# Two causal self-attentions: unread TensorE products ahead of the first transposes and ahead of the first softmax's transposes

## The reference, cut to what matters

```python
def _L0_attn_ref(x, qkv_w, qkv_b, out_w, out_b):
    qkv = (x @ qkv_w + qkv_b).reshape(b, s, 3, h, hd)          # h = 16, hd = 32, s = 64
    q, k, v = (qkv[:, :, 0], qkv[:, :, 1], qkv[:, :, 2])
    logits = jnp.einsum('bqhd,bkhd->bhqk', q, k)
    logits = jnp.where(causal_mask, -jnp.inf, logits) * scale
    att = jax.nn.softmax(logits, axis=-1)
    out = jnp.einsum('bhqk,bkhd->bqhd', att, v).reshape(b, s, d)
    return out @ out_w + out_b

x = x + _L0_xattn_ref(ctx_768, _layernorm(x, axis=-1), ...)    # stage a
x = x + _L0_attn_ref(_layernorm(x, axis=-1), ...)              # stage b
x = x + _L0_ffn_ref(_layernorm(x, axis=-1), ...)               # stage c
x = x + _L1_xattn_ref(_layernorm(x, axis=-1), ctx_768, ...)    # stage d
x = x + _L1_attn_ref(_layernorm(x, axis=-1), ...)              # stage e
x = x + _L1_ffn_ref(_layernorm(x, axis=-1), ...)               # stage f
```

## Time and profile before

| what | us |
|---|---|
| median of 3 runs | 2872.34 |
| these runs | 2870.62 to 2891.36 |
| the profiled execution, its time | 2867.43 |
| the profiled execution, its span | 2865.7 |
| stage b, first statistics to the barrier after it | 1096.6 to 1204.1 |
| stage e, the same | 2290.3 to 2392.8 |

### The profile page before, as it was taken

The page is one execution under the profiler, slowest core; times in us unless marked ns, Lnnn a source line. Parts: engine busy times, 40 slices in busy tenths (PEclk is TensorE's granted clock), DMA queues, the critical chain, the costliest instruction groups (busy, mean ns, idle before and its releaser), DMA issues. The chain is left out here.

```text
span 2865.7 us, 29255 instructions
## 1 busy us (share of the span) xinstructions
PE 2401.2 (84%) x10384; PEld 1468.5 (51%) x10384; DVE 1206.3 (42%) x2242; ACT 738.2 (26%) x1476; POOL 588.5 (21%) x530
## 2 busy tenths in 40 slices
PE   5588988879879778589999977775998776999998
PEld 2435545546456324444444434454464344887886
DVE  4865665665566202410000158775571243311312
ACT  1335334343253200211111134333261012000000
POOL 0330321312303000069997112121000000000000
PEclk9799999999999989689999988776999986998999
DMA  2101101101000031267888463321400012244241
GB/s 79 58 1 49 49 0 48 49 0 48 15 35 11 0 143 66 72 261 303 310 311 318 167 213 111 103 97 36 184 15 0 5 57 120 118 179 172 117 176 73
DMA packets 100219, 298.75 MB, mean 104 GB/s; under 512 B 35824, under 2 KB 63889, under 8 KB 82449
## 3 DMA queue, kind: packets, MB, share of 16 engines
q1 hardware_dynamic: 96096, 285.88, 27.1%
q10 hardware_dynamic: 2736, 7.41, 0.7%
q0 software_dynamic: 1280, 4.20, 0.4%
HBM read 279.05 MB, written 17.30 MB: 103 GB/s over the span
## 5 line engine op out<-in xcount | busy, mean ns | idle before, releaser
L728 PE MATMUL a_mix<-a_probs_T,a_xn 128*128 128x512 f32 (+1 forms) x624 | 271.8, 596 | 5.3 <-ACT a_latent_probs L612 5.3
L425 POOL TENSOR_TENSOR a_xn<-a_xn,a_gain 128x1536 f32<-128x1536 f32 (+1 forms) x32 | 90.4, 2825 | 617.3 <-DVE a_xn L479 616.7
L1514 PE MATMUL c_gate_up<-c_w_wide,c_h_rows 128*128 128x512 f32 x480 | 210.9, 592 | 0.0
L728 PEld LDWEIGHTS a_mix<-a_probs_T,a_xn 128*128 128x128 f32 (+1 forms) x624 | 118.6, 191 | 155.5 <-issue 155.5
L1419 DVE TENSOR_TENSOR c_hidden<-c_silu,c_gate_up 128x512 f32<-128x512 f32 x38 | 26.1, 688 | 353.8 <-PE c_gate_up L1514 343.5
L111 PE MATMUL a_ks<-a_wk_high,a_xn_high 128*128 128x512 f32 x312 | 134.3, 431 | 23.3 <-DVE a_xn_low L459 23.3
L479 DVE TENSOR_SCALAR a_xn<-a_xn,a_mv,a_rstd 128x384 f32<-128x384 f32 (+1 forms) x104 | 146.6, 1465 | 1.2
L1514 PEld LDWEIGHTS c_gate_up<-c_w_wide,c_h_rows 128*128 128x128 f32 x480 | 90.1, 190 | 108.1 <-issue 108.1
L1830 PE MATMUL f_ring<-f_hidden,f_w 128*128 128x160 f32 x1024 | 141.2, 300 | 3.1 <-ACT f_hidden L1758 3.1
L1830 PEld LDWEIGHTS f_ring<-f_hidden,f_w 128*128 128x128 f32 x1024 | 139.3, 190 | 5.1 <-ACT f_hidden L1758 5.1
L1819 PE MATMUL f_ring<-f_picked_T,f_w 128*128 128x160 f32 x1024 | 140.4, 299 | 0.0
(11 more groups left out here) (451 smaller groups left out, 4275.6 us busy)
## 6 DMA issues: line engine op xcount, KB each, us to landing
c_w_wide<-in_L_ffn_W SPq DMA_DIRECT2D x68, 1024.0 KB, 6.9
f_w<-in_L_ffn_W SPq DMA_DIRECT2D x16, 4096.0 KB, 12.0
c_w_down<-in_L_ffn_W SPq DMA_DIRECT2D x34, 1024.0 KB, 7.5
a_xn<-in_ctx SPq DMA_DIRECT2D x24, 768.0 KB
d_context_T<-in_ctx_T SPq DMA_DIRECT2D x24, 768.0 KB, 10.7
d_context<-in_ctx SPq DMA_DIRECT2D x8, 2304.0 KB
mixed_context<-a_mixed SPq DMA_DIRECT2D x24, 256.0 KB, 3.3
a_mixed<-mixed_context SPq DMA_DIRECT2D x1, 6144.0 KB
```

The costliest lines, as they stand in the source:

```text
L425: pool.tensor_tensor(part, part, gain[0:m].unsqueeze(1).to_broadcast([m, hi - lo, DC]), ALU.mult).then_inc(pool_own, 1)
L728: last = pe.matmul(mix[f][:], xn[0:m, par, t, f * P:(f + 1) * P], probs_T[0:m, t, :], start=(t == 0), stop=(t == CT - 1))
L1514: last = pe.matmul(gate_up[2 * (u % 2) + part][:], h[:, k, :], w_wide[:, i % WIDE_RING, k, :], start=(k == 0), stop=(k == KD - 1))
```

## The change

A helper on TensorE issues n products of the identity (stationary, 128 x 128) with `g.hT[:, 0, :]` (moving, 512 columns, float32) into one PSUM bank, each with start and stop set, with no semaphore wait and no signal. Seven stand ahead of the wait for the norm, into `ring[3]`; six stand behind both `pair_scores` calls and ahead of the wait for tile 0's probabilities, into the bank that tile 0's value products write later. Nothing reads either result. Both attentions get them.

```diff
         @block.tensor
         def _(pe):
+            def keep_running(n, out):
+
+                for _ in range(n):
+                    pe.matmul(out, g.ident[:], g.hT[:, 0, :], start=True, stop=True)
+
+            keep_running(7, flat(ring[3]))
             pe.wait_ge(norm.normed, NT)
...
             pair_scores(0)
             pair_scores(1)
             for t in range(NT):
+                if t == 0:
+                    keep_running(6, flat(ring[(R_TILE + 3) % 4]))
                 pe.wait_ge(probs_ready, t + 1)
```

## The result

The changed kernel takes 2885.02 us (median of 20 runs, 2873.45 to 2901.53), the kernel before 2871.5 (20 runs, 2860.99 to 2891.36): ratio 1.0046, 95% interval 1.0028 to 1.0063, that is +13 us with +8 to +18 in the interval. The profiled execution has a span of 2880.5 us. The forecast was 2879.0, +6.7 us: the direction is right, and the size lies just under the interval.

A forecast was written before the change was run, and what follows sets the result against it. TensorE, busy for 84% of the span, was taken to set the time; norms -0.6 (b) and +1.5 (e) and softmaxes +2.9 and +2.9 sum to +6.7 us, from median 2872.34 to 2879.0, range 2870 to 2889.

The forecast's parts named there:

- What one call costs: An added float32 matmul call on TensorE is two instructions: 0.86 us at full clock, 1.71 at half.
- When the clock rises: TensorE's clock reaches full after 2.8 to 5.9 us of work at half clock, middle 4.3.
- Part 1: Stage b's norm: seven calls start at full clock, end 0.6 us late, faster transposes give 1.2 back: -0.6 us.
- Part 2: Stage e's norm: seven calls start at half clock and overrun the gap: +0.8 to +2.35 us, taken as +1.5.
- Parts 3 and 4: Softmaxes of stages b and e: six calls overrun a 2.94 us gap before tile 0's transposes: +2.9 us each.
- I give nothing for tile 1: Softmax, tile 1's transposes: clock falls in some 4.5 us of idle, so no gain; bound -0.9 us each stage.
- A: Rival: the full clock, once reached, holds through the softmax; not slower, -3.3 us, 2869.0; chance 0.12.
- B: Rival: added products do not raise the clock and run at half level throughout; +20.6 us, 2892.9; chance 0.04.
- C: Rival: each added call is one instruction, so the change costs half; -0.85 us, 2871.5; chance 0.04.
- A rule weighed: Norm's transposes: a skill text says transposes don't engage the full clock; the forecast rejected it on the trace; no size.
- nothing for the start of the output projection: Output projection's start, 3.3 us at half clock in stage b: no change counted, may shift either way by 1.6 us.

The follow-up runs named there:

- x2: The changed kernel with the seven norm products taken out, so only the six softmax products stay; ratio 1.0034 against the kernel before.
- x1: The changed kernel with the six softmax products taken out, so only the seven norm products stay; ratio 1.0037 against the kernel before.

## Why the prediction was right, and where it was too low

- What one call costs (two instructions, 0.86 us at full clock, 1.71 at half): right. 52 records more, 6.25 us for fourteen instructions at full clock, 8.61 from half clock, 4.9 and 5.1 us for six more calls.
- When the clock rises, 2.8 to 5.9 us of work with 4.3 as the middle: 4.7 us in e's norm (the level is 0.50 from 2299.0 to 2303.7), and in b's softmax 3.8 us after the calls start (1156.49 to 1160.3), 3.2 forecast. Right.
- Part 1, b's norm, -0.6: -0.6 and, over two profiles each, -0.8. Right for the norm; alone it gives ratio 1.0001, and the stage as a whole is no shorter.
- Part 2, e's norm, +1.5: +1.4. The products ended 8.45 us after the statistics, 8.15 forecast. That the weights' landing would have taken any gain is shown by the run with three calls.
- Parts 3 and 4, +2.9 in each softmax: by VectorE's wait +3.2 and +2.9 in the profile, +2.5 and +2.9 in the second. To the output projection it is +3.05 in b and +2.05 in e, where the level rose ahead of the last tile's transposes (1.09 us, 1.97 before) and gave 0.9 back. Right.
- "I give nothing for tile 1": right, its wait is 2.06 in every execution with the change or with twelve calls.
- The rivals. A fell: the level dropped in the idle behind tile 0, even after twelve calls. What A described is real when the gaps are filled too, and worth 7 us. B fell, as tile 0's transposes ran at full clock; its ground, that 512-column products raise the level "everywhere", was drawn from one place, the output projection of b. C fell by the count.
- "A rule weighed": the window behind the earlier trace rows, in which the last transposes end and no other product starts, is at full clock already, so the level did rise while transposes alone ran. In the changed kernel too, the projections behind b's transposes run at full clock (59 instructions in 25.56 us).

```profile
1104.80:1106.10 1.30, 0.52 (x5) 0.30 (x4) 0.00 (x0) 1.20 (x3) 0.00 (x0) 1.00 0.95 385
```

- The step that was too small is the last of parts 3 and 4, "nothing for the start of the output projection, which ... may shift either way by 1.6". In b it came out +1.8 (18.4 and 18.0 against 17.2 and 15.6). A second term was missing from the sum altogether: in e the first scores fall behind the clock's drop, +0.7. With these two the parts are -0.8 + 1.4 + 3.05 + 2.05 + 1.8 + 0.7 = 8.2 us, what was found in b and e, against 6.7.
- The rest, 12 to 13 us less 8.2, lies in stages that the change does not touch, and the forecast had no term for them. By the means of the two executions c and d are 3.4 us longer and f 2.1, which with the 8.2 makes 13.8. Two executions of each would be too few to call that an effect; all thirteen say more (us):

| profiled executions | b, output projection to next stage | c and d | e, output projection to next stage | f |
|---|---|---|---|---|
| before, twice | 17.2, 15.6 | 1086.2, 1086.5 | 16.2, 16.1 | 472.9, 472.6 |
| the change, twice | 18.4, 18.0 | 1091.7, 1087.9 | 16.2, 16.2 | 474.8, 474.9 |
| norm's seven alone | 18.3 | 1088.1 | 18.5 | 470.6 |
| softmax's six alone | 18.0 | 1087.9 | 18.5 | 470.6 |
| twelve | 18.6 | 1088.6 | 17.6 | 473.1 |
| b's seven alone | 18.3 | 1088.2 | 16.2 | 472.5 |
| e's seven alone | 15.7 | 1086.0 | 16.2 | 474.8 |
| three in e | 15.7 | 1085.6 | 18.4 | 470.5 |
| six between the scores | 15.6 | 1086.6 | 16.2 | 472.5 |
| sized to the gaps | 15.6 | 1086.4 | 16.1 | 472.9 |
| the same, c and f too | 15.7 | 1086.0 | 16.2 | 473.3 |

The six executions in which stage b has the change's products in their places (or twelve of them) have both the slow output projection of b and a longer c and d (1087.9 and more); the other seven have neither (1086.6 at most, and 17.2 once for the output projection). So 1.3 us or more in c and d come with the products in b; that is a match over thirteen executions, not a mechanism. The first execution's 1091.7 is an outlier among them, 4 us of it between the first and the second norm of d. For f the trace shows the place: its last 16 products take 14.10 us in both executions of the change, 8.50 in both of before, and they start 3 to 4 us earlier in the stage. Of the other nine, only the run with e's seven alone and the one with products in c and f have this (14.10, 14.07).

```profile
2857.90 14.10 PE L1853 MATMUL f_acc<-f_y,f_put_back 128*128 128x512 f32 x16 [0.93 <-DVE f_y L1742]
```

Why the level falls at these places in one execution and not in another stays open, and the interval of the ratio, +8 to +18, does not test a surplus of this size.

## What to carry to other kernels

Work that only keeps TensorE's clock up paid here where it started while the clock was full and ended before the data came; at half clock each instruction takes twice as long (0.86 us against 0.43), and what overruns the gap lies in front of the work it is to help. Count the instructions that a float32 product turns into before sizing it, and look at what else lands at the same point (here the weights, in stage e). Filling one gap bought nothing here while the next was left open (ratios 1.0001 and 0.9997); filling all of them up to the last tiles gave 0.9975. And look behind the place that was changed: what is gained or lost there can come back, with either sign, in a stage that nobody touched.

## What was not expected of the hardware

- Single executions of one kernel lie 30 us apart (2860.99 to 2891.36 for the kernel before, in one series), and much of it in a stage that none of the kernels changed: stage a ended between 1094.6 us (x2) and 1112.3 (x1) in the profiles. A change of 0.2% can't be read from a single total; it can be read stage by stage, if the stages behind it are looked at too.
- Where the clock changes falls differently from one execution to the next, and a few us of shift ahead of it move costs to places that the change does not touch: the output projection of b started with 3.3, 5.5 or no us at half clock.
- Thirty-two products of 8 columns at the head of stage f take 7.00 us at half clock in the kernel before. They take 4.14 us behind the added products, but also 4.2 to 4.8 us in six executions that have nothing added in stage f (4.21 in the changed kernel): their time goes with the level at which they start, and that differs between executions of kernels whose stage f is the same.
